# Two halved bias tables moved from the head of VectorE's sequence to just before the first maxima, with a new work order for all engines

## The chip, the cores and the metric

The kernel runs on one core of one Trainium2 chip. Its time is the device time of one execution in microseconds (us). The core has TensorE (PE: matmuls and transposes, its results go to PSUM), VectorE (DVE), ScalarE (ACT), GpSimd (POOL) and SyncE (SP, which here only issues DMAs). Each engine works through its own list of instructions in order, and waits on semaphores for the others.

## What is computed

One transformer layer on x of shape 2 x 1024 x 128, in float32:

```python
x = x + attn(layernorm(x), Wq, Wk, Wv, q_gamma, ..., Wo, bo)   # 16 heads of 8, causal,
                                                               # layernorm per head on q and k, rope, softmax
x = x + ffn(layernorm(x), ...)
# ffn: gate = softmax(x @ gate_w.T); the best 2 of 4 groups, then the best 2 of 16 experts
h1 = einsum('td,edi->tei', xf, We1) + be1
h3 = einsum('td,edi->tei', xf, We3) + be3
yo = einsum('tei,eid->ted', silu(h1) * h3, We2) + be2
y  = einsum('te,ted->td', combine, yo)
z  = silu(xf @ ws1 + bs1) * (xf @ ws3 + bs3) @ ws2 + bs2        # two shared experts
```

All 16 experts are computed for all tokens, as 8 pairs and one unit for the shared experts (9 units of 128 rows), and weighted afterwards. The silu is made of a tanh, with input and one bias halved: tanh((a + b1) / 2), and (c + b3) / 2. The tables of halved biases are `b1h` and `b3h`, 128 x 9 each.

## The kernel before

The 2048 tokens are four tiles x = 0 to 3 of 512 (tiles 0 and 1 are the first halves of the two batches). Attention runs in 16 groups a = 0 to 15 (4 heads of one tile each). A group's maxima come first: `max` (PE, scores of queries against keys), `maxred` (DVE, reduction out of PSUM), `mneg` (POOL), `mturn` (PE), `mcopy` (ACT), `mrow` (SP). Then `scores` (PE), `exp` (ACT), `pv` (PE), `leave` (ACT), `oT` (PE), `oT_read` (DVE). A tile whose attention is done goes through `onT`, `proj` (PE), `proj_read`, `norm2` (DVE), `norm2_apply` (ACT), `x2T` (PE), `gate` (PE), `gate_read`, `route1` to `route3` (DVE), `cT` (PE), `cT_read` (ACT), `cstore` and `cload` (SP: the weights of the experts go to DRAM and come back spread over the partitions), and the units of its experts: `moeV`, `moeU` (PE), `moe_v`, `moe_t` (ACT), `moe_a` (DVE), `moe_g` (POOL), `moe_h` (POOL; for tile 3 `moe_h_dve` on DVE) and `moe_y` (PE, sum over the units), then `y_leave` (ACT), `yturn` (PE), `final` (DVE) and `store` (SP).

There is no scheduler. A text table `ORDER` of 1323 words gives one total order of these stages; each engine walks through it and emits those that are its own (`for kind, arg in SCHEDULE`). A word such as `max.8.2@01` also names the PSUM banks that the stage fills. Moving a word moves the stage within its engine's sequence, and its waits with it.

Ahead of the table's stages SP issues all loads in a fixed list (L501 to L531): the attention weights, the rope tables and biases (`ld_rope`), the masks, tile 1 of x, four padding loads of the stacked keys and queries, tiles 2 and 3 of x, and last the 14 loads of the experts (`ld_moe`), of which the shared bias `bs2` is the last. Tile 0 of x is loaded through ACT's queue (L787). SP's first stage of the table is `stack.0.0.0` (L489), a DMA of the first bf16 parts of the rotated queries.

The head of the sequence goes: `norm.0` (DVE, L1017 on: statistics, a Newton iteration for the square root in ops of 128x4, and the normalised tile) waits only for tile 0 of x; `xT.0`, `qkv.0` to `qkv.3` (PE) and their reads (ACT); `tables.0` (DVE, L1147) waits for `ld_rope`; `norm.1`; `headsum.0`, `headrstd.0`, `rope.0` (DVE); `qT.0`, `kT.0` (PE), their parts and stacks; then the first `max`. For tile 1 POOL makes the rope products (`rope_pool.1`, `rope_join.1`), and `xbo` (POOL, L970) adds the output bias to a tile. The stage `halved` (DVE, L1160 and L1161) makes `b3h` and `b1h`:

```python
dve.wait_ge(ld_moe, 16 * N_MOE)
dve.tensor_scalar(b3h[:, :], b3[:, :], 0.5, None, ALU.mult)
dve.tensor_scalar(b1h[:, :], b1[:, :], 0.5, None, ALU.mult).then_inc(consts, 1)
```

`consts` is waited for by ACT ahead of `moe_v.0.0` and `cT_read.0` alone. In the kernel before `halved.0` is the first word of the table.

Of the kernel before, what the change touches and what calls it, by code (L numbers as in the profile page):

```python
# [134 lines left out]
qkv.10@4 qkv_read.9 qkv.11@3 rope_pool.1 qkv_read.10 stack_act.0.1.2 qkv_read.11 headsum.2 max.0.0@45 max.0.1@23  # L135
maxred.0.0 max.0.2@01 maxred.0.1 max.0.3@45 rope_join.1 maxred.0.2 max.0.4@23 maxred.0.3 max.0.5@01 maxred.0.4
max.1.0@45 maxred.0.5 max.1.1@23 maxred.1.0 xbo.2 norm_apply.3 max.1.2@01 qT.1@6 maxred.1.1 max.1.3@45 mneg.0
maxred.1.2 qT_lead.1 rstd_pool.2 max.1.4@23 stack.1.0.0 maxred.1.3 max.1.5@01 maxred.1.4 mturn.0@5 xT.3@4 mcopy.0
maxred.1.5 xT_read.3 mrow.0 max.2.0@23 kT.1@5 maxred.2.0 qkv.12@4 kT_lead.1 qT_rest.1 max.2.1@01 qkv_read.12
stack.1.1.0 max.2.2@23 maxred.2.1 qkv.13@6 qkv.14@4 stack.1.0.1 maxred.2.2 qkv_read.13 max.2.3@01 kT_rest.1 qkv_read.14  # L140
qT_low.1 max.2.4@23 qkv.15@6 maxred.2.3 stack.1.1.1 kT_low.1 max.2.5@45 qkv_read.15 maxred.2.4 scores.0.0@01 xbo.3
stack.1.0.2 exp.0.0 maxred.2.5 stack.1.1.2 scores.0.1@23 mneg.1 exp.0.1 scores.1.0@01 headsum.3 rope_pool.2 mturn.1@6
max.3.0@45 exp.1.0 max.3.1@23 maxred.3.0 pv.0 mcopy.1 maxred.3.1 mrow.1 scores.1.1@01 max.3.2@45 exp.1.1 scores.2.0@23
maxred.3.2 exp.2.0 max.3.3@01 max.3.4@45 maxred.3.3 pv.1 maxred.3.4 scores.3.0@23 pv.2 exp.3.0 mneg.2 max.3.5@01
rstd_pool.3 leave.0 mturn.2@6 maxred.3.5 max.4.0@45 mcopy.2 scores.3.1@23 mrow.2 maxred.4.0 exp.3.1 oT.0@6 max.4.1@01
oT_read.0 max.4.2@45 maxred.4.1 scores.4.0@23 pv.3 exp.4.0 maxred.4.2 max.4.3@01 scores.4.1@23 maxred.4.3 max.4.4@45
exp.4.1 maxred.4.4 scores.5.0@01 scores.6.0@23 exp.5.0 pv.4 exp.6.0 mneg.3 max.4.5@45 scores.6.1@01 rope_join.2
maxred.4.5 pv.5 exp.6.1 scores.7.0@23 leave.1 mturn.3@6 max.5.0@45 mcopy.3 max.5.1@01 maxred.5.0 exp.7.0 mrow.3 pv.6
# [5 lines left out]
exp.11.0 scores.12.0@01 maxred.6.4 rope_join.3 pv.10 mcopy.5 exp.12.0 pv.11 mrow.5 max.6.5@45 leave.3 max.7.0@23
maxred.6.5 scores.12.1@01 stack.2.0.1 oT.3@6 exp.12.1 maxred.7.0 max.7.1@45 stack.2.0.2 oT_read.3 scores.13.0@01
scores.13.1@23 stack.2.1.2 maxred.7.1 mneg.6 exp.13.0 qT.3@6 exp.13.1 pv.12 qT_lead.3 scores.14.0@01 max.7.2@45
qT_rest.3 exp.14.0 max.7.3@23 pv.13 maxred.7.2 qT_low.3 pv.14 max.7.4@01 maxred.7.3 leave.4 onT.0@6 maxred.7.4
max.7.5@45 onT_read.0 scores.15.0@23 proj.0@6 exp.15.0 maxred.7.5 scores.15.1@01 proj_read.0 scores.16.0@23 exp.15.1
norm2.0 mturn.6@5 oT.4@6 mneg.7 exp.16.0 max.8.0@01 mturn.7@4 mcopy.6 pv.15 mcopy.7 mrow.6 max.8.1@23 kT.3@5 mrow.7
kT_lead.3 maxred.8.0 norm2_apply.0 stack.3.1.0 maxred.8.1 max.8.2@01 x2T.0@4 oT_read.4 kT_rest.3 max.8.3@23 x2T_read.0  # L160
moeV.0.0@4 maxred.8.2 kT_low.3 stack.3.1.1 moeU.0.0@5 moe_v.0.0 maxred.8.3 stack.3.1.2 max.8.4@01 moe_t.0.0 moeV.0.1@4
maxred.8.4 max.8.5@23 moe_v.0.1 moe_a.0.0 gate.0@6 maxred.8.5 moe_g.0.0 max.8.6@45 max.8.7@01 maxred.8.6 moeU.0.1@3
gate_read.0 moeV.0.2@2 moe_t.0.1 maxred.8.7 moe_y.0.0 moe_v.0.2 moe_a.0.1 max.8.8@45 gate_exp.0 max.8.9@01 maxred.8.8
# [10 lines left out]
exp.22.0 moe_y.0.5 moe_h.0.7 exp.22.1 moe_y.0.6 moe_g.0.8 moe_y.0.7 moe_h.0.8 scores.23.0@01 scores.24.0@23 exp.23.0
stack.3.0.1 pv.21 exp.24.0 moe_y.0.8 stack.3.0.2 stack.3.0.0 scores.24.1@01 y_leave.0 scores.25.0@23 pv.22 exp.24.1
exp.25.0 yturn.0@5 scores.25.1@01 final.0 pv.23 exp.25.1 scores.26.0@23 store.0 max.9.3@45 leave.7 maxred.9.3
max.9.4@01 exp.26.0 pv.24 maxred.9.4 max.9.5@45 oT.7@6 maxred.9.5 pv.25 oT_read.7 scores.26.1@01 scores.27.0@23
exp.26.1 max.9.6@45 onT.1@6 maxred.9.6 exp.27.0 pv.26 onT_read.1 max.9.7@45 scores.27.1@01 maxred.9.7 proj.1@6 exp.27.1
# [1075 lines left out]
```

## Time and profile before

| | us |
|---|---|
| median of 3 runs | 449.93 (449.13 to 450.18) |
| the profiled execution, its own time | 447.54 |
| its span, first to last instruction | 445.7 |
| PE busy | 355.9 (80%) |
| DVE busy | 316.7 (71%) |
| ACT busy | 267.3 (60%) |
| POOL busy | 151.8 (34%) |

The profiled execution lies 2.4 us under the median, and 1.8 us of its time lie outside the span. Rows of the trace have the start of an instruction or a merged group in us from the span's start, its length, engine, source line and operation, what it writes and reads, how many, and in brackets how long the engine had been idle and what released it. SPq and ACTq are the issue of a DMA.

### The profile page before, as it was taken

To read this page: it belongs to the slowest core of one execution; us is meant where nothing else is said; L and a number is where in the kernel's file an instruction comes from. 1 tells how busy PE (TensorE), PEld (TensorE's weight loads), DVE (VectorE), ACT (ScalarE), POOL (GpSimd) and SP (SyncE) were. 2 spreads that over 40 slices of the span, in tenths; PEclk is the share of its full clock that TensorE was granted. 3 is DMA by queue.
4 is the path that set the end of the run, shared out by engine and by line. 5 is a ranking of instruction groups with operands and counts; after the bars stand their busy time and mean duration, and the time that the engine had idled before them with its cause. 6 is when DMAs were issued, how large, how long until landed. Compare 5 with 4: busy or idle time off the path is not lost.

```text
span 445.7 us, 8177 instructions
## 1 busy us (share of the span) xinstructions
PE 355.9 (80%) x2999; PEld 154.1 (35%) x2999; DVE 316.7 (71%) x619; ACT 267.3 (60%) x395; POOL 151.8 (34%) x182
## 2 busy tenths in 40 slices
PE   1005445889898999999978998989978699999895
PEld 1002222535454343434422333333432233344332
DVE  0027999997979997527897876888897961136954
ACT  1004433477677477677758268767856479957670
POOL 0003179788871223920135720000000001557252
PEclk9999756799999899999989999999979999999999
DMA  4970040130130202630000800000000001700081
GB/s 122 212 130 1 0 118 24 48 98 2 41 85 26 72 1 53 142 94 3 0 0 13 181 2 1 3 2 25 2 2 0 4 1 28 166 1 0 1 189 50
DMA packets 26424, 21.69 MB, mean 49 GB/s; under 512 B 9201, under 2 KB 22162, under 8 KB 26322
## 3 DMA queue, kind: packets, MB, share of 16 engines
q1 hardware_dynamic: 24994, 20.12, 19.4%
q10 hardware_dynamic: 1392, 1.05, 0.9%
q8 instruction: 25, 0.41, 0.4%
q14 instruction: 13, 0.11, 0.1%
HBM read 13.56 MB, written 1.18 MB: 33 GB/s over the span
## 4 chain that ended last, share of the span: by engine, by line
PE 42%; DVE 39%; SPq 7%; issue 4%; ACT 4%; DMA 2%; POOL 1%; DVEq 0%; ACTq 0%
PE psum L687 11%; DVE mx_diag L1072 11%; DVE mx_full L1072 7%; PE psum L666 6%; PE psum L722 6%; PE psum L733 5%; PE psum L640 4%; PE psum L614 3%; PE psum L596 2%; ACT probs L795 2%; SPq L523 2%; DVE mv L1144 2%; DVE nr L1011 2%; DVE nr L1012 2%; DMA comb_b<-combine_scratch 1%
## 5 line engine op out<-in xcount | busy, mean ns | idle before, releaser
L795 ACT ACTIVATE probs<-psum 128x1024 f32<-128x1024 f32 x144 | 141.6, 1022 | 55.8 <-PE psum L614 29.9
L1072 DVE TENSOR_REDUCE mx_diag<-psum 128x4 f32<-128x512 f32 (+2 forms) x96 | 96.0, 1040 | 18.4 <-PE psum L640 17.9
L1072 DVE TENSOR_REDUCE mx_full<-psum 128x2 f32<-128x1024 f32 x64 | 75.9, 1219 | 12.6 <-PE psum L640 12.3
L994 POOL TENSOR_TENSOR mh<-mh,mv 128x512 f32<-128x512 f32 x36 | 45.4, 1270 | 98.2 <-DVE mv L1144 98.2
L687 PE MATMUL psum<-probs,v_ones 128*9 128x512 f32 (+3 forms) x768 | 78.0, 497 | 1.0 <-ACT probs L795 0.8
L722 PE MATMUL psum<-x2T,w 128*128 128x512 f32 x144 | 72.3, 629 | 2.9 <-ACT mv L832 1.6
L640 PE MATMUL psum<-k_st,q_st 62*128 62x512 bf16 (+3 forms) x384 | 58.4, 337 | 7.2 <-DVE mx_full L1072 4.9
L666 PE MATMUL psum<-q_st,k_st 64*128 64x512 bf16 (+3 forms) x384 | 54.5, 331 | 8.3 <-DVE mx_full L1072 4.0
L614 PE MATMUL psum<-masks 64*128 64x128 bf16 (+2 forms) x896 | 50.7, 213 | 11.7 <-DVE mx_diag L1072 7.7
L1144 DVE SCALAR_TENSOR_TENSOR mv<-psum,b,mv 128x512 f32<-128x512 f32 x36 | 26.5, 747 | 35.1 <-ACT mh L844 34.9
L614 PEld LDWEIGHTS psum<-masks 64*128 64x128 bf16 x896 | 32.7, 95 | 44.7 <-DVE mx_diag L1072 21.2
L952 POOL CAST negmax<-mx_diag 128x16 bf16<-128x16 f32 x16 | 3.1, 196 | 109.2 <-DVE mx_diag L1197 81.1
L733 PE MATMUL psum<-mh,w 128*128 128x512 f32 x72 | 36.2, 614 | 2.7 <-DVE mh L478 1.6
L722 PEld LDWEIGHTS psum<-x2T,w 128*128 128x128 f32 x144 | 25.8, 196 | 31.7 <-issue 16.2
L666 PEld LDWEIGHTS psum<-q_st,k_st 64*128 64x128 bf16 x384 | 16.5, 94 | 55.6 <-ACT probs L795 32.6
L478 POOL TENSOR_TENSOR mh<-mh,comb_b 128x512 f32<-128x512 f32 x24 | 29.9, 1268 | 6.7 <-DMA comb_b<-combine_scratch 6.0
L596 PE MATMUL psum<-ident,sq 128*128 128x128 f32 x16 | 3.5, 361 | 35.4 <-DVE sq L1032 27.8
L841 ACT ACTIVATE mh<-psum,b1h 128x512 f32<-128x512 f32 x36 | 24.7, 686 | 11.7 <-PE psum L722 11.7
L832 ACT ACTIVATE mv<-psum,b3h 128x512 f32<-128x512 f32 x36 | 24.4, 678 | 7.1 <-PE psum L722 7.0
L640 PEld LDWEIGHTS psum<-k_st,q_st 62*128 62x128 bf16 x384 | 19.0, 97 | 27.3 <-DVE mx_full L1072 12.5
L844 ACT ACTIVATE mh<-mh 128x512 f32<-128x512 f32 x36 | 22.7, 630 | 1.1
L687 PEld LDWEIGHTS psum<-probs,v_ones 128*9 128x9 f32 x768 | 13.7, 89 | 26.6 <-issue 20.3
(146 smaller groups left out, 395.4 us busy)
## 6 DMA issues: line engine op xcount, KB each, us to landing
comb_b<-combine_scratch SPq DMA_DIRECT2D x32, 256.0 KB, 5.4
q_st<-parts SPq DMA_DIRECT2D x24, 128.0 KB, 2.3
k_st<-parts SPq DMA_DIRECT2D x18, 128.0 KB, 2.3
w<-in_We SPq DMA_DIRECT2D x3, 512.0 KB
k_st<-in_c_pad SPq DMA_DIRECT2D x2, 512.0 KB, 8.5
out<-xs SPq DMA_DIRECT2D x4, 256.0 KB, 2.3
xs<-in_x SPq DMA_DIRECT2D x3, 256.0 KB, 10.4
k_st<-parts ACTq DMA_DIRECT2D x6, 128.0 KB, 2.7
```

Source lines behind the costliest of these rows:

```text
L478: engine.tensor_tensor(h, h, comb_b[:, u, :], ALU.mult).then_inc(weighted, 1)
L614: return pe.matmul(dst, masks[r, slot, :], blocked, start=start, stop=stop, skip_group_check=True)
L640: last = pe.matmul(w[:, par, i * keys:(i + 1) * keys], q_st[r, x % 2, 2 * g + m, q0:q0 + P], k_st[r, b, 2 * g + m, k0:k0 + keys], start=(w ...
L666: last = pe.matmul(w[:, par, col:col + cols], k_st[rows(par), b, 2 * g + m, kt * P:(kt + 1) * P], q_st[rows(par), x % 2, 2 * g + m, q0:q0 ...
L687: last = pe.matmul(acc[32 * j:32 * j + VC, q0:q0 + cols], v_ones[:, b, kt, G * g + j, :], probs[:, n % P_RING, j % 2, col:col + cols], sta ...
L722: pe.matmul(w, (w1 if kind == "moeU" else w3)[:, unit(n), :], x2T[:, x % 2, :], start=True, stop=True).then_inc(work_full, 1)
L733: last = pe.matmul(y, w2[:, unit(n), :], mh[:, at % T_RING, :], start=(n == 0), stop=(n == UNITS - 1), skip_group_check=True)
L795: act.activation(probs[:, n % P_RING, :, :], wpair("scores", (s, i)), ACT.Exp, scale=SCALE).then_inc(exp_done, 1)
L841: act.activation(t, wbank("moeU", (x, n)), ACT.Tanh, bias=b1h[:, unit(n):unit(n) + 1], scale=0.5).then_inc(act_t, 1)
L994: pool.tensor_tensor(t, t, mv[:, at % V_RING, :], ALU.mult).then_inc(gate_done, 1)
L1072: dve.tensor_reduce(dst[:, a % 2, qt, :, pairs[0]:pairs[0] + nm], w, AX.X, ALU.max, negate=True).then_inc(max_free, 1)
L1144: dve.scalar_tensor_tensor(out=v, in0=wbank("moeU", (x, n)), scalar=b1[:, unit(n):unit(n) + 1], in1=v, op0=ALU.add, op1=ALU.mult).then_inc ...
```

## The change

No instruction is added or removed. `halved.0` leaves the head of the table and stands behind `norm.3`, ahead of `headsum.2` and the first `maxred`. The rest of the table is a new order from there on. Up to `halved.0` every engine has the same sequence as before.

```diff
 ORDER = """
-halved.0 ones.0 ones.1 norm.0 weights.0@6 weights_read.0 weights2.0@5 weights2_read.0 tables.0 xbo.0 xT.0@6 xT_read.0
+ones.0 ones.1 norm.0 weights.0@6 weights_read.0 weights2.0@5 weights2_read.0 tables.0 xbo.0 xT.0@6 xT_read.0 norm.1
...
+qkv.10@4 qkv_read.9 qkv.11@3 rope_pool.1 stack_act.0.1.2 qkv_read.10 qkv_read.11 halved.0 headsum.2 max.0.0@45
...
+moe_v.3.4 final.2 moe_g.3.2 cT.3@2 moe_a.3.3 store.2 moeU.3.4@3 cT_read.3 moe_g.3.3 cstore.3 moeV.3.5@5 moe_t.3.4
```

VectorE at the head of the program (`-` is the kernel before, `+` the changed one; L1019 and L1022 are the first ops of `norm.0`):

```order
 L1153 MEMSET combT 17x512
 L1154 MEMSET psum 128x512
-L1160 TENSOR_SCALAR b3h<-b 128x9
-L1161 TENSOR_SCALAR b1h<-b 128x9
 L1019 BN_STATS stats<-xs 128x6 x4
 L1022 BN_AGGR mean_var<-stats 128x2 x4
```

`norm.0` now follows the two memsets directly, and the wait for the experts' loads has gone from there.

VectorE where the two ops stand now (L1013 and L1036 end `norm.3`, L1041 is `headsum.2`, L1072 the first maxima):

```order
 L1013 SCALAR_TENSOR_TENSOR rstd<-nr,seed 128x4
 L1036 SCALAR_TENSOR_TENSOR shift<-mean_var,rstd 128x4
+L1160 TENSOR_SCALAR b3h<-b 128x9
+L1161 TENSOR_SCALAR b1h<-b 128x9
 L1041 TENSOR_REDUCE ssum<-sq 128x128
 L1072 TENSOR_REDUCE mx_diag<-psum 128x4 x2
```

GpSimd beside that place (L457 and L460 are the end of `rope_pool.1`, L970 is `xbo.2`, L468 and L469 are `rope_join.1`):

```order
 L457 TENSOR_TENSOR sq<-qk,g_cos 128x1024
 L460 TENSOR_TENSOR roped<-qk,g_sin 128x16x32 x2
+L970 TENSOR_TENSOR xs<-xs,bo_b 128x512
 L468 TENSOR_TENSOR sq<-sq,g_add 128x1024
 L469 TENSOR_TENSOR roped<-roped,sq 128x1024
-L970 TENSOR_TENSOR xs<-xs,bo_b 128x512
```

`xbo.2` now comes ahead of `rope_join.1`.

PE near the end of the program, before (L697 is `proj.3`, L596 of w_raw is `x2T.3`, L705 is `gate.3`, L713 is `cT.3`, L722 are `moeV` and `moeU`, L733 and L737 `moe_y`):

```order
L697 MATMUL psum<-w_o,o_normT 128x128 x4
L722 MATMUL psum<-x2T,w 128x512 x6
L733 MATMUL psum<-mh,w 128x512 x3
L596 MATMUL psum<-ident,w_raw 128x128 x4
L733 MATMUL psum<-mh,w 128x512
L705 MATMUL psum<-w_o,x2T 128x16 x4
L722 MATMUL psum<-x2T,w 128x512 x3
L733 MATMUL psum<-mh,w 128x512
L722 MATMUL psum<-x2T,w 128x512 x5
```

The same place after (L596 of yT is `yturn.2`):

```order
L722 MATMUL psum<-x2T,w 128x512 x3
L733 MATMUL psum<-mh,w 128x512 x2
L737 MATMUL psum<-combT,b 128x512
L733 MATMUL psum<-mh,w 128x512 x2
L596 MATMUL psum<-ident,w_raw 128x128 x4
L733 MATMUL psum<-mh,w 128x512 x2
L705 MATMUL psum<-w_o,x2T 128x16 x4
L733 MATMUL psum<-mh,w 128x512 x2
L722 MATMUL psum<-x2T,w 128x512 x4
L733 MATMUL psum<-mh,w 128x512
L722 MATMUL psum<-x2T,w 128x512 x2
L596 MATMUL psum<-ident,yT 128x128 x4
```

Between `x2T.3` and `cT.3` PE has 11 `moeV`, `moeU` and `moe_y` stages of tile 3 and tile 2 besides one ahead of the gate before; now it has 13 and `yturn.2` there, two of the `moe_y` ahead of the gate. `moe_y.2.0`, which stood ahead of the end of attention, comes after it. `yturn.2`, `final.2` and `store.2` come ahead of `cstore.3` on their engines; before they came behind the last `cload`.

In the stretch of tile 0's second norm, PE had `mturn.6 oT.4 max.8.0 mturn.7 pv.15 max.8.1 kT.3 max.8.2` between `scores.16.0` and `x2T.0`. Now it has `pv.15 scores.16.1 scores.17.0 mturn.6 max.8.0 max.8.1 pv.16 max.8.2 mturn.7 pv.17 max.8.3` there. The units of tile 0's experts, which stood among maxima and scores, stand closer together, and `oT.4` and `kT.3` behind them.

## Rows read from the trace of the kernel before

**Rows 1.** The page: busy time, then busy tenths in 40 equal slices.
```profile
PE 355.9 (80%) x2999; PEld 154.1 (35%) x2999; DVE 316.7 (71%) x619; ACT 267.3 (60%) x395; POOL 151.8 (34%) x182
...
DVE  0027999997979997527897876888897961136954
```
**Rows 2.** Waits, first 60 us: engine and work, releaser, us in total, times, longest.
```profile
DVE b3h L1160 <- DMA b<-in_bs: 28.7, 1, 28.7
```
**Rows 3.** Timeline, head: start, length, engine, line, operation.
```profile
0.72 0.47 ACTq L787 DMA_DIRECT2D xs<-in_x  x1
...
6.37 0.43 SPq L508 DMA_DIRECT2D bo_b<-in_bo  x1
...
7.32 0.43 SPq L511 DMA_DIRECT2D xs<-in_x  x1
...
29.25 0.33 SPq L531 DMA_DIRECT2D b<-in_bs  x1
30.73 0.17 DVE L1160 TENSOR_SCALAR b3h<-b 128x9 f32<-128x9 f32 x1 [28.69 <-DMA b<-in_bs]
...
30.88 0.86 DVE L1019 BATCH_NORM_STATS2 stats<-xs 128x6 f32<-128x128 f32 x4
...
35.40 0.17 DVE L1149 COPY gb_rot<-gb 128x16 f32<-128x16 f32 x1
...
38.17 0.87 DVE L1019 BATCH_NORM_STATS2 stats<-xs 128x6 f32<-128x128 f32 x4
...
42.16 0.16 DVE L1036 SCALAR_TENSOR_TENSOR shift<-mean_var,rstd 128x4 f32<-128x4 f32 x1
...
43.96 1.22 DVE L1041 TENSOR_REDUCE ssum<-sq 128x128 f32<-128x1024 f32 x1 [1.64 <-ACT v_ones L815]
```
**Rows 4.** DMA issues: KB each, median us from issue to landing; then line 511 alone.
```profile
xs<-in_x ACTq DMA_DIRECT2D x1, 256.0 KB, 3.6
bo_b<-in_bo SPq DMA_DIRECT2D x1, 64.0 KB, 4.1
out<-xs SPq DMA_DIRECT2D x4, 256.0 KB, 2.3
...
DMA to landing us min/median/max: 5.3/10.4/10.7
```
**Rows 5.** Timeline, first stack DMA to the first maxima.
```profile
57.68 27.70 SPq L489 DMA_DIRECT2D q_st<-parts  x9
...
67.55 2.34 POOL L454 TENSOR_TENSOR qk<-qk,hrstd 128x1024 f32<-128x1024 f32 x1
67.64 2.27 DVE L1012 TENSOR_TENSOR nr<-nr,rstd 128x4 f32<-128x4 f32 x1
...
74.07 1.97 POOL L468 TENSOR_TENSOR sq<-sq,g_add 128x1024 f32<-128x1024 f32 x1
...
75.25 12.12 DVE L1072 TENSOR_REDUCE mx_diag<-psum 128x4 f32<-128x512 f32 x13
...
78.42 1.27 POOL L970 TENSOR_TENSOR xs<-xs,bo_b 128x512 f32<-128x512 f32 x1
```
**Rows 6.** Timeline near the end: a one-input VectorE op beside GpSimd.
```profile
400.62 1.26 POOL L478 TENSOR_TENSOR mh<-mh,comb_b 128x512 f32<-128x512 f32 x1
...
401.08 0.83 DVE L1028 TENSOR_SCALAR rstd<-mean_var 128x4 f32<-128x4 f32 x1
```
**Rows 7.** Stretches: length, busy PE, PEld, DVE, ACT, POOL, clock, DMA share, GB/s.
```profile
140.00:150.00 10.00, 7.92 (x38) 3.23 (x38) 9.05 (x28) 5.68 (x12) 1.57 (x3) 0.83 0.24 70
150.00:160.00 10.00, 9.65 (x68) 4.44 (x66) 9.65 (x15) 5.43 (x10) 2.52 (x2) 1.00 0.04 12
...
340.00:350.00 10.00, 7.48 (x108) 3.02 (x108) 8.68 (x17) 4.96 (x6) 0.42 (x2) 1.00 0.01 3
```
**Rows 8.** Timeline, tail of tile 3.
```profile
411.93 1.02 PE L733 MATMUL psum<-mh,w 128*128 128x512 f32 x2
...
421.64 0.60 PE L713 MATMUL psum<-ident,lg 128*16 128x128 f32 x4 [1.14 <-DVE lg L1138]
```

More of the change, by code:

```diff
@@ L134 @@
 kT_rest.0 stack.0.0.1 xT.2@6 norm.3 stack_act.0.1.1 xT_read.2 qT_low.0 qkv.8@6 qkv.9@5 qkv_read.8 kT_low.0 stack.0.0.2
[L135 to L148, printed above, removed]
@@ L154 @@
[L154 to L163, printed above, removed]
@@ L174 @@
[L174 to L178, printed above, removed]
@@ new lines @@
+norm_apply.3 qT.1@6 maxred.1.3 rstd_pool.2 max.1.5@01 maxred.1.4 mturn.0@5 qT_lead.1 kT.1@4 mcopy.0 stack.1.0.0
+maxred.1.5 kT_lead.1 max.2.0@23 xT.3@5 maxred.2.0 max.2.1@01 xT_read.3 mrow.0 qT_rest.1 max.2.2@23 qkv.12@5 maxred.2.1
+stack.1.1.0 qkv.13@6 qkv_read.12 maxred.2.2 max.2.3@01 qkv_read.13 qkv.14@5 stack.1.0.1 maxred.2.3 max.2.4@23
+qkv_read.14 qT_low.1 kT_rest.1 qkv.15@6 max.2.5@01 maxred.2.4 qkv_read.15 xbo.3 stack.1.1.1 maxred.2.5 kT_low.1
+scores.0.0@23 stack.1.0.2 exp.0.0 headsum.3 scores.0.1@01 mneg.1 stack.1.1.2 rope_pool.2 exp.0.1 scores.1.0@23
@@ new lines @@
+mneg.8 scores.21.1@01 moe_h.0.8 scores.22.0@23 exp.21.1 mturn.8@5 pv.20 mcopy.8 moe_y.0.7 exp.22.0 mrow.8 moe_y.0.8
+leave.6 scores.22.1@01 y_leave.0 pv.21 exp.22.1 max.9.0@45 max.9.1@23 maxred.9.0 pv.22 scores.23.0@01 maxred.9.1
+max.9.2@45 exp.23.0 stack.3.0.1 oT.6@6 maxred.9.2 scores.24.0@23 scores.24.1@01 exp.24.0 stack.3.0.2 pv.23 oT_read.6
+stack.3.0.0 yturn.0@5 leave.7 exp.24.1 scores.25.0@23 final.0 oT.7@6 exp.25.0 max.9.3@45 oT_read.7 store.0 pv.24
+maxred.9.3 scores.25.1@01 scores.26.0@23 exp.25.1 onT.1@6 max.9.4@45 exp.26.0 pv.25 maxred.9.4 onT_read.1
@@ new lines @@
+moe_y.1.1 maxred.10.10 moe_h.1.3 max.10.11@23 moe_h.1.4 max.10.12@45 maxred.10.11 scores.34.1@01 moe_y.1.2 exp.34.1
+maxred.10.12 moe_h.1.5 max.10.13@23 scores.35.0@01 maxred.10.13 pv.34 moe_h.1.6 exp.35.0 mmin.10 max.11.0@45
+max.11.1@23 moe_h.1.7 maxred.11.0 max.11.2@01 moe_y.1.3 mneg.10 maxred.11.1 moe_y.1.4 moe_h.1.8 moe_y.1.5 maxred.11.2
+moe_y.1.6 max.11.3@45 max.11.4@23 maxred.11.3 max.11.5@01 moe_y.1.7 maxred.11.4 moe_y.1.8 mturn.10@5 maxred.11.5
+y_leave.1 scores.35.1@23 mcopy.10 yturn.1@4 exp.35.1 mrow.10 max.11.6@01 final.1 maxred.11.6 scores.36.0@23 store.1
@@ L252 @@
+moeV.3.7@3 moe_t.3.6 cload.3.2 moe_g.3.5 moeU.3.7@2 cload.3.3 moe_v.3.7 moeV.3.8@4 moe_a.3.6 moe_t.3.7 moeU.3.8@3
+moe_g.3.6 moe_h_dve.3.1 moe_v.3.8 moe_h_dve.3.2 moe_y.3.1 moe_t.3.8 moe_h_dve.3.3 moe_h_dve.3.4 moe_h_dve.3.5 moe_y.3.2
+moe_h_dve.3.6 moe_a.3.7 moe_y.3.3 moe_a.3.8 moe_g.3.7 moe_y.3.4 moe_y.3.5 moe_g.3.8 moe_h_dve.3.7 moe_y.3.6
+moe_h_dve.3.8 moe_y.3.7 moe_y.3.8 y_leave.3 yturn.3@5 final.3 store.3
 """
```

186 lines of the change are left out of this document (97 added, 89 removed).

## The prediction, made before the changed kernel ran

> **What bounds the kernel now.** I read the page's busy shares first, then the waits of the first 60 us, then the timeline of the head, and only then the stretches and the tail. The page shows PE busy for 80% of the span and DVE for 71%, so no single engine fills it; but the DVE row of the slices is 0 for the first two slices (22 us) and 2 in the third [rows 1]. The kernel is PE-bound once attention runs, and nothing-bound at its head. The waits name the cause: DVE stood 28.7 us at `b3h`, for the load of the last shared bias [rows 2]. The timeline shows that load issued by SP at 29.25 as the last of the fixed list, `b3h` at 30.73, and `norm.0` behind it at 30.88 [rows 3]. Tile 0 of x, which is all that `norm.0` needs, had been issued at 0.72 and took 3.6 us to land [rows 3, 4]: it lay there from 4.3 on. All further work hangs on `norm.0`, so the wait is on the path in full. What the reader should see is that two ops of 0.17 us hold up the program because their engine works in order, not because anybody needs them: their readers are the experts' units, which need a whole tile's attention first.
>
> **Part 1, the wait leaves the head.** I follow the DVE chain to `headsum.0` (43.96), the first op that needs both DVE's and ACT's work [rows 3]. `norm.0` starts at 0.72 + 3.6 = 4.3 in place of 30.88. It took 35.40 - 30.88 = 4.5 us and the last of its output some 0.1 more: done at 8.9. `tables.0` waits for the rope loads; the last, `bo_b`, is issued at 6.37 and lands 4.1 later, at 10.5 [rows 3, 4]. So a new wait of 1.6 us appears here. The tables took 38.17 - 35.40 = 2.8 us: 13.3. `norm.1` needs tile 1 of x, issued at 7.32; of the three loads of line 511 it is the first and has the minimum of 5.3 us, since the four padding loads come behind it: 12.6, so it does not wait [rows 3, 4]. It took 42.32 - 38.17 = 4.15 us: 17.45. On the other side ACT finished its reads of `qkv.0` to `qkv.3` at 43.96, which is 8.5 us behind `norm.0`: 17.4. `headsum.0` stood 1.64 us idle for ACT before [rows 3]; that slack swallows the new wait for the tables. So `headsum.0` starts at 17.5 in place of 43.96, which is **26.5 us earlier**.
>
> From there to the first maxima at 75.25 [rows 5] the sequences are the same, and the question is which absolute time they run into. SP's list is done at 29.25 + 0.33 = 29.6 [rows 3]. The first stack DMA was issued at 57.68 [rows 5] and moves to 31.2, 1.6 us behind SP's list and 0.5 behind the landing at 30.7. Tiles 2 and 3 of x are issued at about 11 and land 10.7 us later at most [rows 4], near 22, ahead of `norm.2` (after the stacks' start, beyond 30). So nothing of the gain is taken back here. The cover is thin, though: without those 1.6 us of margin every microsecond more is lost. Bounds of this term: 24.5 (SP's list or x late by 2 us) to 26.6 (30.88 - 4.3).
>
> **Part 2, the two ops where they stand now.** They come at 74.2 on the old clock, some 48 on the new: the loads are in since 30.7, there is no wait. Alone they cost 2 x 0.17 = 0.3 us, and DVE is on the path, being busy without a gap into the maxima from 75.25 [rows 5]. But GpSimd works beside them on 128x1024 operands. An op of 128x4 on DVE that starts under such an op lasts until it ends: 2.27 us, against 2.34 of GpSimd's `qk` [rows 5]. That one has two inputs; the nearest row for a one-input TENSOR_SCALAR is 0.83 us, begun 0.46 after a GpSimd op of 1.26 and ending with it [rows 6]. So they block as well. In the new order GpSimd runs `xbo.2` (1.27 us [rows 5]) at 74.07 where `rope_join.1` (1.97) began. `b3h` then waits some 1.2 us, and `b1h` either slips through behind it or waits 1.97 more. Bounds 0.3 to 3.5; I take 2.0, between the two outcomes. It costs on DVE; PE waits for the maxima there anyway.
>
> The Trainium skill, page "SBUF — State Buffer", section "SBUF: two separate sides", says that GpSimd and VectorE share one port pair under an exclusive lock, and that a VectorE op is locked out when it is in a 2-port mode or has two SBUF inputs. If our one-input op ran in no such mode, the price would be the 0.3 us; the row of 0.83 us speaks for the lock.
>
> **Part 3, the new order, middle.** The same stages at the same lengths; only gaps can change. The clearest gap is that of tile 0's second norm: PE was busy 7.92 of 10 us from 140 on and 9.65 in the next stretch [rows 7], so about 1.7 us are lost while `x2T.0` waits. The new order has two `scores` and two `pv` more in that place. I take -1.0 (0 to -1.7). Elsewhere PE's idle share in such a stretch goes up to 2.5 us in the last row there [rows 7], and I can't rank the rest: the closer row of tile 0's experts costs ACT about what PE needs for them. I put 0 with bounds of -4 to +4, some two such stretches closed or opened.
>
> **Part 4, the tail.** A `moe_y` takes 1.02 us, four transposes 0.60 [rows 8]. Between `x2T.3` and `cT.3` PE has two more `moe_y` and `yturn.2`: 2.64 us; `cT.3` waited 1.14 us for DVE's routing [rows 8], so 1.5 us remain. One `moe_y` has left the work ahead of attention's end, -1.0. And `store.2` now is issued just ahead of `cstore.3`: 256 KB that take 2.3 us to land [rows 4] stand before the small store on which the experts' weights depend. Bounds 0 to 2.3; I take 0.5, since `final.2` is ready at about the time of `cT.3`. Sum of the tail +1.0 (-0.5 to +3).
>
> The Trainium skill, page "DMA: Bandwidth & Descriptors", section "Queues, rings and completion order", says that descriptors of one issuing engine are consumed in ring order on each DMA engine. By that the 256 KB are served first and the price would be nearer to the upper bound, +2.3 in place of +0.5; no row here has the two together.
>
> **Sum.** -26.5 + 2.0 - 1.0 + 1.0 = -24.5 us. The profiled execution, 447.54 (span 445.7), would go to 423.0 (span 421.2). The median lies 2.4 above it; from the median 449.93 the forecast is **425.4**.
>
> **Rivals.** *A, the new order fits better than I can see* (it fills gaps of the size of [rows 7] in several stretches): another -5 to -9, 416 to 420. For it: PE idles in nearly every stretch. Against: each such gap ends on DVE, which is busy 71%.
> *B, it fits worse*: another +5.5 to +12, 431 to 437, if tile 0's experts in a closer row starve PE. For it: each unit passes ACT, DVE and GpSimd in turn. Against: PE's work for a unit is as long as ACT's.
> *C, the head gives less*: if the stack DMAs or SP's list are late, or the port holds both ops and more, 3 to 8 us of the gain go: 428 to 433.
> *D, no change*: the freed time is lost at a point that does not move, such as the stacks waiting for the whole load list at a later landing. It would need the list to end near 57; it ended at 29.6 [rows 3]. 450.
> *E, slower*: the experts of tile 0 stand in PE's queue in a row, and the maxima and scores behind them wait. PE idles when a unit's chain (two products, ACT, DVE, GpSimd) is slower than PE's own work for it. If each of the 36 units cost 0.75 us of PE (DVE's op per unit, unhidden), that is 27 us and more than the head gives: 452 or more. It decides from there on, when PE's idle time of today in the attention part nearly doubles. Against: only tile 0's units have clearly moved together, and `mv` and `mh` have several buffers, so that units overlap.
>
> **How the numbers follow.** Forecast (419.5 to 430.5): 0.70. A: 0.13. B: 0.07. C beyond the forecast's range: 0.06. D: 0.015. E: 0.025. The forecast's range adds the bounds roughly in squares: 1.5 for the head, 1.6 for the port, 4 for the middle, 1.8 for the tail, about 4.9 to either side; with the near part of A and of B and C, 419 to 431 holds about 8 in 10. Differences within 0.2% (0.9 us) can't be told from no change: faster 0.96, same 0.015, slower 0.025.
>
> **What would show it.** In the profile after, `norm.0` starts near 4.3 and nothing waits for `b<-in_bs`; DVE waits about 1.6 us at the tables for `bo_b`; `headsum.0` is at 17.5, the first stack DMA at 31.2, the first maxima at about 50.8 rather than 48.8; L1160 and L1161 last together 1 to 3 us. PE's stretch about `x2T.0` is busy 9 of 10. `cT.3` has no wait for DVE, and `combine_scratch` lands later than 1.6 us after issue if `store.2` is ahead. If the span from the first maxima to the end is over 5 us from 445.7 - 75.25 = 370.5, the middle was wrong; if `headsum.0` is later than 20, the head was.

## The result: the head gave what was forecast, the middle gave far more

| kernel | median, us | lowest to highest | profiled execution | its span | its mean clock |
|---|---|---|---|---|---|
| before, beside after | 449.97 | 449.13 to 450.18 (4) | 447.54 | 445.7 | 0.950 |
| after | 416.95 | 416.74 to 419.32 (4) | 416.74 | 414.9 | 0.954 |

The ratio is 0.929 (95% interval 0.926 to 0.932): 33.0 us faster between the medians, 30.8 between the two profiled spans. The forecast was 24.5 us, 425.4, with 419.0 as its lower end. The result lies 2 us below that range, where rival A had put its 416 to 420.

The page of after, busy shares and then DVE and the clock in 40 slices (10.4 us each). Against [rows 1], DVE has work from the first slice on and PE fills 85% of the span; the sum of PE's busy time fell from 355.9 to 352.3 us with the same 2999 matmuls. The clock row has a dent in its first slices and one 8 behind it.

```profile
PE 352.3 (85%) x2999; PEld 153.8 (37%) x2999; DVE 314.9 (76%) x619; ACT 267.0 (64%) x395; POOL 151.3 (36%) x182
...
DVE  4899998878899963789988977698998741265753
...
PEclk9865859999999999999999999999989999999999
```

The same row of before has its dent from the fifth slice on, and behind it 8, 8 and 7, which I had passed over:

```profile
PEclk9999756799999899999989999999979999999999
```

The head, which answers to [rows 3]. The timeline of DVE in after, and SP's queue: start, length, engine, line, operation, and in brackets the wait.

```profile
4.28 0.87 DVE L1019 BATCH_NORM_STATS2 stats<-xs 128x6 f32<-128x128 f32 x4 [2.25 <-DMA xs<-in_x]
...
10.83 0.17 DVE L1149 COPY gb_rot<-gb 128x16 f32<-128x16 f32 x1 [1.94 <-DMA bo_b<-in_bo]
...
13.63 0.86 DVE L1019 BATCH_NORM_STATS2 stats<-xs 128x6 f32<-128x128 f32 x4
...
17.70 1.21 DVE L1041 TENSOR_REDUCE ssum<-sq 128x128 f32<-128x1024 f32 x1
```

```profile
29.87 0.33 SPq L531 DMA_DIRECT2D b<-in_bs  x1
31.37 1.88 SPq L489 DMA_DIRECT2D q_st<-parts  x3
```

`norm.0` starts at 4.28 (said: 4.3), DVE waits 1.94 us at the tables for `bo_b` (said: 1.6), `norm.1` doesn't wait, `headsum.0` starts at 17.70 (17.5), the first stack DMA is issued at 31.37 (31.2). The two halved ops, where they stand now, with GpSimd beside them:

```profile
47.82 1.24 DVE L1160 TENSOR_SCALAR b3h<-b 128x9 f32<-128x9 f32 x1
48.97 0.16 DVE L1161 TENSOR_SCALAR b1h<-b 128x9 f32<-128x9 f32 x1
49.05 1.20 DVE L1041 TENSOR_REDUCE ssum<-sq 128x128 f32<-128x1024 f32 x1
50.17 10.38 DVE L1072 TENSOR_REDUCE mx_diag<-psum 128x4 f32<-128x512 f32 x11
```

```profile
47.76 1.26 POOL L970 TENSOR_TENSOR xs<-xs,bo_b 128x512 f32<-128x512 f32 x1
```

The first maxima are at 50.17 in place of 75.25: 25.1 us. Up to here the sum was right within a microsecond. From there to the end of the span before took 370.4 us and after takes 364.7. The prediction had named its own test for this: over 5 us from 370.5, and the middle was wrong. It is 5.8.

### The profile page after: what moved, and what is told of

The parts are those of the page before. It is cut to its first block, busy times and chain, and to the rows that moved or that the text cites. A ratio compares the mean times of both kernels' runs of the same rounds, so it can differ in the third digit from the quotient of the medians.

```text
span 414.9 us, 8178 instructions
## 1 busy us (share of the span) xinstructions
PE 352.3 (85%) x2999; PEld 153.8 (37%) x2999; DVE 314.9 (76%) x619; ACT 267.0 (64%) x395; POOL 151.3 (36%) x182
## 4 chain that ended last, share of the span: by engine, by line
PE 45%; DVE 35%; ACT 6%; issue 6%; DMA 3%; POOL 2%; SPq 2%; DVEq 0%; ACTq 0%; POOLq 0%
PE psum L687 14%; PE psum L666 8%; DVE mx_diag L1072 7%; DVE mx_full L1072 6%; PE psum L733 5%; PE psum L614 5%; PE psum L640 4%; PE psum L722 4%; ACT probs L795 4%; PE psum L596 4%; DVE mv L1144 2%; DVE nr L1012 2%; POOL mh L994 2%; DVE nr L1011 2%; DMA comb_b<-combine_scratch 2%
## 5 line engine op out<-in xcount | busy, mean ns | idle before, releaser
L1072 DVE TENSOR_REDUCE mx_diag<-psum 128x4 f32<-128x512 f32 (+2 forms) x96 | 95.7, 1038 | 19.0 <-PE psum L640 17.9
L1072 DVE TENSOR_REDUCE mx_full<-psum 128x2 f32<-128x1024 f32 x64 | 75.6, 1217 | 16.9 <-PE psum L640 16.7
L722 PE MATMUL psum<-x2T,w 128*128 128x512 f32 x144 | 69.1, 606 | 1.5 <-ACT mv L832 0.8
L1144 DVE SCALAR_TENSOR_TENSOR mv<-psum,b,mv 128x512 f32<-128x512 f32 x36 | 26.3, 746 | 30.1 <-ACT mh L844 30.0
L733 PE MATMUL psum<-mh,w 128*128 128x512 f32 x72 | 35.4, 612 | 3.7 <-DVE mh L478 2.8
L722 PEld LDWEIGHTS psum<-x2T,w 128*128 128x128 f32 x144 | 25.0, 189 | 30.1 <-issue 18.3
L605 PE MATMUL psum<-w_qkv,xnT 128*128 128x384 f32 x32 | 17.7, 708 | 2.9 <-ACT xnT L801 2.9
```

Source lines behind the costliest of these rows:

```text
L722: pe.matmul(w, (w1 if kind == "moeU" else w3)[:, unit(n), :], x2T[:, x % 2, :], start=True, stop=True).then_inc(work_full, 1)
L733: last = pe.matmul(y, w2[:, unit(n), :], mh[:, at % T_RING, :], start=(n == 0), stop=(n == UNITS - 1), skip_group_check=True)
L1072: dve.tensor_reduce(dst[:, a % 2, qt, :, pairs[0]:pairs[0] + nm], w, AX.X, ALU.max, negate=True).then_inc(max_free, 1)
L1144: dve.scalar_tensor_tensor(out=v, in0=wbank("moeU", (x, n)), scalar=b1[:, unit(n):unit(n) + 1], in1=v, op0=ALU.add, op1=ALU.mult).then_inc ...
```

## Where the rest came from: the two traces side by side

I took the gain (start or end in before less that in after) at steps that both orders have. First maxima 25.1; fifth attention block left (136.6 against 113.5) 23.1; `proj_read.0` 22.9; tile 0's experts done (the eighth block left, 198.7 against 170.3) 28.3; the thirteenth, 324.9 against 297.1, 27.9; the fourteenth, 351.9 against 320.6, 31.4; `x2T.3` read, 407.5 against 375.3, 32.2; the end 30.8. So there are two jumps: 5.4 us in the stretch of tile 0's second norm and experts, 3.5 us in that of tile 2's second norm.

In both places the clock column differs. Stretches of before (length, busy PE, PEld, DVE, ACT, POOL, then the granted clock, DMA share, GB/s):

```profile
144.00:146.00 2.00, 1.17 (x6) 0.74 (x6) 1.97 (x4) 1.17 (x4) 0.00 (x0) 0.84 0.17 44
146.00:148.00 2.00, 1.77 (x6) 0.62 (x5) 1.97 (x4) 0.58 (x1) 0.61 (x1) 0.50 0.54 157
148.00:150.00 2.00, 2.00 (x6) 0.61 (x4) 1.57 (x2) 0.81 (x2) 0.54 (x1) 0.80 0.50 143
...
328.00:330.00 2.00, 0.82 (x6) 0.32 (x4) 2.00 (x3) 0.64 (x1) 0.00 (x0) 0.92 0.00 0
330.00:332.00 2.00, 1.80 (x14) 0.82 (x14) 1.86 (x6) 1.63 (x3) 0.00 (x0) 0.50 0.03 8
332.00:334.00 2.00, 2.00 (x10) 0.15 (x9) 1.87 (x8) 1.61 (x2) 0.00 (x0) 0.50 0.00 0
```

and PE's timeline in the first of them:

```profile
144.77 0.39 PE L640 MATMUL psum<-k_st,q_st 62*128 62x512 bf16 x2 [1.80 <-DVE mx_full L1072]
145.22 1.01 PE L596 MATMUL psum<-ident,w_raw 128*128 128x128 f32 x4
...
147.00 2.84 PE L722 MATMUL psum<-x2T,w 128*128 128x512 f32 x4 [0.23 <-ACT x2T L801]
```

Read it like this: PE stands 1.80 us for DVE; from 145.4 on the clock is at 0.50 (1.2 of 2.4 GHz), four transposes take 1.01 us in place of 0.63 to 0.66, and four expert products take 2.84 us, 0.71 each (the clock is back at 148.8, within them). After has in the same place a pause too, but of 0.61 us, and a clock of 1.00; its experts' products take 0.49 each:

```profile
122.94 0.63 PE L596 MATMUL psum<-ident,w_raw 128*128 128x128 f32 x4 [0.61 <-ACT maxT L906]
...
124.52 1.07 PE L705 MATMUL psum<-w_o,x2T 128*128 128x16 f32 x8
125.43 1.96 PE L722 MATMUL psum<-x2T,w 128*128 128x512 f32 x4
```

The pause costs once; what follows it costs again, without PE being idle there. A caution on the two jumps: only 3.4 us at half clock lie in the first of them, and 6.8 against 3.4 in the second, so that the clock column alone can't fill both; a later section comes back to this. Hence two theories. **K**: the gain over the forecast is time at half clock that no longer occurs, and whoever keeps PE busy in the pause gets it in any order. **G**: it is the gaps themselves that the order closes. And before these, whether it is the order at all (**O**), or the shift by 25 us that moved the work to other places of whatever sets the clock (**S**).

## Experiments

**Head and order apart.** In the order of before, one word moved:

```diff
-halved.0 ones.0 ones.1 norm.0 ...
+ones.0 ones.1 norm.0 ... kT_rest.0 stack.0.0.1 xT.2@6 norm.3 halved.0 stack_act.0.1.1 ...
```

> The order of before with one word moved: the two halved ops stand behind norm.3 in place of at the head. Theory O (what I missed is the new order: it closes holes in PE's row, and with them half-clock stretches): this kernel has the head's gain alone, 25.1 us at the first maxima, and nothing more, so 423 to 426 us; its trace keeps stretches of granted clock 0.50 after the second norms of tiles 0 and 2. Theory S (the shift itself did it: the same order, begun 25 us earlier, runs with fewer half-clock stretches): 417 to 419 us, and the stretches at 0.50 are gone with the old order too.

Measured 426.92 us (423.79 to 428.76), 22.9 less than the 449.77 of before beside it.

```diff
-ones.0 ones.1 norm.0 weights.0@6 ... qkv_read.11 halved.0 headsum.2
+halved.0 ones.0 ones.1 norm.0 weights.0@6 ... qkv_read.11 headsum.2
```

> The new order with the two halved ops put back at the head. Theory O: the order alone is worth the 5.7 us that the profiled spans show behind the first maxima, up to 8 if the medians' part is the order's too: 442 to 444 us. Theory S: the order is worth nothing by itself, 448 to 450 us.

Measured 441.93 us (441.20 to 442.97), 7.8 less (ratio 0.983, 0.978 to 0.987). So O holds and S falls: the order by itself is worth 7.8 us, at the old place of the halved ops. The two parts add up to 30.7 of the 33.0. The first came out 1 us above what O had said, and its executions lie 5 us apart; the next sections give a likely reason for both.

**Which half of the order.** After's order up to `leave.7`, then before's, and the reverse, both with the halved ops moved.

> Halved moved; the new order up to leave.7 (the experts of tile 0 done), and from there the old one. Theory O: the gain at leave.7 was 28.3 us and at the first maxima 25.1, so this part of the order is worth 3.2: about 421.5 us, 3 below the old order with halved moved, and no half-clock stretch near the x2T.0 hole, but one near the second norm of tile 2. Theory S: like the old order with halved moved.

Measured 423.77 us (423.24 to 424.89), 2.3 above the 421.5 expected. And its trace has the clock at 0.50 from 126.2 to 129.7, behind `x2T.0`, where none was expected: up to `leave.7` its sequence is that of after, whose clock stood at 1.00 there.

> Halved moved; the old order up to leave.7, and from there the new one. Theory O: the rest of the order is worth 5.7 - 3.2 = 2.5 us: about 422.5 us, with a half-clock stretch behind x2T.0 and a shorter one near the second norm of tile 2. Theory S: like the old order with halved moved.

Measured 420.04 us (418.91 to 421.19). Against the 426.92 of the old order the first half is worth 3.2, which is the difference expected, and the second 6.9, where I expected 2.5. Together that is 10.0, and from 426.92 to after it is 10.0. The halves add up, but their sizes are not those of the two profiled executions.

**The half clock itself.** In the old order with the halved ops moved: nine matmuls of 128x512 in bf16 that compute nothing, in the pause ahead of `max.8.2`. They write the bank that `x2T.0` fills next and overwrites.

```diff
+KEEP = {("max", (8, 2)): ("x2T", 0, 9)}
 for kind, arg in SCHEDULE:
+    if (kind, arg) in KEEP:
+        name, at, count = KEEP[kind, arg]
+        spare = fill(name, at)
+        for _ in range(count):
+            pe.matmul(spare, ident_bf[:, :], masks[:, 0:4, :].rearrange("p n q -> p (n q)"),
+                      start=True, stop=True, skip_group_check=True)
```

> The old order with halved moved, and 9 spare bf16 matmuls (128x512, about 0.21 us each, into the bank that x2T.0 fills next, which overwrites them) just ahead of max.8.2, where PE waited 1.80 us for DVE at 121.2 and behind which the clock stood at 0.50 from about 120.9 to 128.6. Theory K (PE's pause costs little, the half clock behind it costs half of its length): the clock stays at 1.00 there, 7.7 us of it, and the time falls by 3 to 4 us against the old order with halved moved, 426.9 to about 423.5, although work was added. Theory G (the pause itself is what the order closes): nothing changes, or PE's queue comes some 0.1 us later: 427.

Measured 422.77 us (422.40 to 423.18): 4.15 less than the 426.92 without them (3.7, if each is taken against the kernel before beside it), and all of its executions are below all of the other's. Work was added, nothing moved. PE in the old order with halved moved, first without and then with the spare matmuls (line 746, lines behind it are 7 further down):

```profile
121.18 0.39 PE L640 MATMUL psum<-k_st,q_st 62*128 62x512 bf16 x2 [1.80 <-DVE mx_full L1072]
121.62 1.11 PE L596 MATMUL psum<-ident,w_raw 128*128 128x128 f32 x4
...
123.50 2.90 PE L722 MATMUL psum<-x2T,w 128*128 128x512 f32 x3 [0.23 <-ACT x2T L801]
```

```profile
118.82 2.11 PE L746 MATMUL psum<-masks 128*128 128x512 bf16 x9
120.86 0.39 PE L640 MATMUL psum<-k_st,q_st 62*128 62x512 bf16 x2
121.23 0.66 PE L596 MATMUL psum<-ident,w_raw 128*128 128x128 f32 x4
...
122.65 1.96 PE L722 MATMUL psum<-x2T,w 128*128 128x512 f32 x4 [0.34 <-ACT x2T L808]
```

and the clock of the stretches that follow, again without and with:

```profile
120.00:122.00 2.00, 0.77 (x4) 0.50 (x5) 2.00 (x2) 1.57 (x5) 0.00 (x0) 0.88 0.02 6
122.00:124.00 2.00, 1.77 (x7) 0.94 (x6) 1.93 (x6) 0.59 (x1) 0.21 (x1) 0.50 0.70 197
124.00:126.00 2.00, 2.00 (x3) 0.67 (x2) 1.97 (x2) 0.41 (x1) 0.94 (x1) 0.50 0.39 110
126.00:128.00 2.00, 2.00 (x5) 0.38 (x4) 0.16 (x1) 0.96 (x2) 0.00 (x0) 0.50 0.31 95
```

```profile
120.00:122.00 2.00, 1.97 (x13) 0.82 (x10) 1.97 (x4) 1.25 (x5) 0.00 (x0) 1.00 0.17 45
122.00:124.00 2.00, 1.66 (x5) 0.69 (x5) 1.97 (x4) 0.72 (x2) 0.60 (x1) 1.00 0.57 164
124.00:126.00 2.00, 2.00 (x8) 0.45 (x6) 2.00 (x3) 1.79 (x3) 0.55 (x1) 1.00 0.25 66
126.00:128.00 2.00, 1.85 (x15) 1.29 (x14) 2.00 (x3) 0.69 (x1) 0.55 (x1) 1.00 0.45 131
```

The expert products go from 0.97 us each to 0.49. K holds in this place: from the first maxima to the eighth block left, the two traces take 126.1 us (10.2 of it at half clock, 3.4 of them at 97) and 122.7 us (none). The Trainium skill, page "TensorE: Matmul & The Clock Gate", section "Why this matters for your kernels", warns of idle gaps between bursts that let the clock fall. The rows agree that it falls behind idle time. The longest single pause here, 1.80 us, is shorter than the gaps that the page names.

The same nine matmuls in the kernel before itself:

> The kernel before, with nothing moved, and 9 spare matmuls ahead of max.8.2, as in the kernel with the old order and halved moved. Its clock stood at 0.50 from about 145.3 to 149.6 behind this pause, and the same edit took 4.15 us off the old order with halved moved. Theory K: 2 to 4 us faster than before, 446 to 447.5. Theory G: 449 to 450.

Measured 447.51 us (445.58 to 448.53, 10 executions) beside 448.99 (17 executions); ratio 0.9967 (0.9945 to 0.9990). That is 1.5 us, with an interval of 0.5 to 2.5, and less than the 2 to 4 I gave it. The stretch there was 3.4 us long, so half of it, 1.7, is what K should have said; 4.15 had been measured where it was twice as long. The two profiled spans are equal (445.9 and 445.7), although this execution has 3.4 us less at half clock (10.2 against 13.6, one stretch at 354 being new). So the factor of a half doesn't hold for this pair of traces.

**More spare work, in the maxima.** There PE has no free bank ahead of its pauses, so the spare matmuls write the bank of the step itself, once it is free:

```diff
+KEEP = {("max", (8, 2)): ("x2T", 0, 9), ("max", (14, 6)): ("max", (14, 6), 2), ("max", (14, 7)): ("max", (14, 7), 2),
+        ("scores", (59, 0)): ("scores", (59, 0), 2), ("scores", (59, 1)): ("scores", (59, 1), 2)}
```

> As the kernel with 9 spare matmuls, and 2 more (0.43 us) behind the bank wait of each of max.14.6, max.14.7, scores.59.0 and scores.59.1, where PE stood 0.4 to 0.6 us for DVE four times and the clock then stood at 0.50 for 7.5 us (305.9 to 313.3). Theory K: another 3 us less, about 420.5. Theory G: 427, or up to 1 us more for the spare work.

Measured 422.36 us (421.75 to 422.87), only 0.4 less than without these eight; K had said 3. The half clock near 305 is gone in the trace, but one at 217 is there in its stead. That the spare work, which now stands between the maxima, delays DVE is my reading of the rest; no run here shows it by itself.

```diff
+KEEP = {("scores", (59, 0)): ("scores", (59, 0), 3), ("max", (14, 8)): ("max", (14, 8), 3)}
```

> The new order as in after, with 3 spare matmuls (0.64 us) behind the bank wait of scores.59.0 and of max.14.8, the two pauses of 0.69 and 0.78 us ahead of its only half-clock stretch in the middle (301.9 to 305.3). Theory K: this stretch goes, -1.7 us, 415.2. Theory G: 417.0 or 0.5 more.

Measured 416.72 us (415.05 to 420.88), against 416.95 of after: no difference, and so inconclusive. Its four executions took 420.88, 415.05, 417.66 and 415.78 us at mean clocks of 0.935, 0.955, 0.943 and 0.959. In the profiled one, the slowest, the stretch near 302 is gone. But behind `x2T.0`, on rows that are those of after up to 124.9 us (0.36 us later), the clock fell where it had not in after:

```profile
123.30 0.63 PE L596 MATMUL psum<-ident,w_raw 128*128 128x128 f32 x4 [0.61 <-ACT maxT L913]
...
124.56 0.39 PE L640 MATMUL psum<-k_st,q_st 62*128 62x512 bf16 x2 [0.31 <-DVE mx_full L1079]
124.88 1.54 PE L705 MATMUL psum<-w_o,x2T 128*128 128x16 f32 x8
```

The eight products that took 1.07 us in after take 1.54 here, with the same pauses ahead; the clock stood at 0.50 from 125.3 to 132.1. Two more traces have after's instructions up to here: that with the order of before from `leave.7` on and that with `store.2` moved (below); in both the clock fell too, at 126.2 and at 125.9. So the pauses make a fall possible, not certain; it differs from execution to execution of the same instructions.

**One number for all kernels.** For every profiled execution I took the time from the first maxima to the end of the span, and the sum of (1 - clock) / 0.5 over stretches of 1 us (from 16 us behind the first maxima, where the head's slow start is over, to 6 us ahead of the end), which is the time at half clock. At half clock a product takes twice its time (0.97 against 0.49 us above), so a PE that bounds loses half of it; where another engine bounds, less is lost.

| kernel | first maxima to end | at half clock | first less half of second |
|---|---|---|---|
| before | 370.4 | 13.6 | 363.6 |
| old order, halved moved | 376.8 | 26.4 | 363.6 |
| new then old | 372.6 | 17.1 | 364.1 |
| old then new | 368.9 | 13.7 | 362.1 |
| new order, halved at the head | 364.7 | 3.4 | 363.0 |
| after | 364.7 | 3.4 | 363.0 |
| old order, halved moved, 9 spare | 370.0 | 10.2 | 364.8 |
| the same and 8 more | 370.6 | 6.8 | 367.2 |
| after, 6 spare | 369.3 | 11.3 | 363.6 |
| before, 9 spare | 370.4 | 10.2 | 365.3 |
| new order, halved behind `maxred.0.4` | 364.7 | 3.4 | 363.0 |
| after, `store.2` moved | 367.8 | 13.7 | 361.0 |
| new order, halved behind `maxred.0.4`, 12 spare | 364.2 | 3.4 | 362.5 |
| the same, 11 spare, one pause earlier | 364.1 | 3.4 | 362.4 |

The times from the first maxima differ by 13 us, the last column, for the eight kernels without spare work, by 3. By this sum the old and the new order are 0.6 us apart (363.6 and 363.0), and 5.1 of the order's 5.7 us are clock. But the factor of a half is no more than a rule. Pairs of traces of one order give it directly: before and the old order with halved moved 6.4 us for 12.8, so 0.5; after and its variant with 6 spare 4.6 for 7.9, 0.6 (1.3 us of spare work in it); after and that with `store.2` moved 3.1 for 10.3, 0.3; before and the same with 9 spare nothing for 3.4. With 0.3 in place of 0.5 the clock's share of the 5.7 us is 3.1. So at least about half of the order's gain is clock, perhaps nearly all; these single executions don't say more.

Cut at the eighth block left, the traces show where the order itself counts. From the first maxima to there before took 123.4 us with 3.4 at half clock, before with 9 spare 122.9 with none, and after 120.2 with none. Of these 3.2 us 0.5 went with the half clock, and 2.7 stayed with the clock at 1.00 on both sides: this part is the order's own, by G. From there to the read of `x2T.3` it was 208.8 us with 10.3 at half clock in before and 204.9 with 3.4 in after; there the 6.9 us fewer at half clock are worth 2.1 to 3.4 of the 3.9.

**The price of the two ops beside GpSimd.** The new order with them behind the fifth read of maxima, `maxred.0.4`:

```diff
-qkv_read.10 qkv_read.11 halved.0 headsum.2 max.0.0@45 ...
+qkv_read.10 qkv_read.11 headsum.2 max.0.0@45 ... max.0.5@01 maxred.0.4 halved.0
```

> The new order with the two halved ops four maxima reads later, behind maxred.0.4, where GpSimd's joined rope (2.34 us) is still running or just over. If the 1.24 us that L1160 took beside GpSimd's xbo.2 was on the path, and GpSimd is idle where they stand now, the gain is about 1.1 us: 415.8. If they fall under the 2.34 us op, they hold DVE up to 2.3 us, and the time is 0 to 1 us over after.

Measured 415.98 us (415.03 to 417.07). The time alone doesn't part it from after; the trace does:

```profile
47.40 0.16 DVE L1036 SCALAR_TENSOR_TENSOR shift<-mean_var,rstd 128x4 f32<-128x4 f32 x1
47.48 1.21 DVE L1041 TENSOR_REDUCE ssum<-sq 128x128 f32<-128x1024 f32 x1
48.61 4.67 DVE L1072 TENSOR_REDUCE mx_diag<-psum 128x4 f32<-128x512 f32 x5
53.20 0.16 DVE L1160 TENSOR_SCALAR b3h<-b 128x9 f32<-128x9 f32 x1
53.27 0.16 DVE L1161 TENSOR_SCALAR b1h<-b 128x9 f32<-128x9 f32 x1
```

Both ops now take 0.16 us, and `headsum.2` follows `norm.3` at once. In after they held it up from 47.82 to 49.05, so they cost 1.2 us there and cost 0.15 here (53.20 to 53.35): 1.1 us to be had.

**The store in the tail.** In the new order `store.2` moved behind `cload.3.3`.

> The new order with store.2 moved behind cload.3.3. If its 256 KB ahead of the small store hold this one up, the time from the issue of combine_scratch to the issue of its first read back falls from the 1.88 us of after towards the 1.66 of before, and by no more than 0.3 us; if the queue had cost what I allowed at most, 2.3 us, after would have shown 3.9, so that is out already. The time itself: 415 to 417.5.

One execution, 419.29 us at a clock of 0.941, which says nothing of an edit of this size. In its trace the first read back of the experts' weights is issued 1.71 us behind the small store, in after 1.88:

```profile
390.80 0.39 SPq L557 DMA_DIRECT2D out<-xs  x1
391.47 0.60 SPq L545 DMA_DIRECT2D combine_scratch<-combT  x1
393.35 5.20 SPq L553 DMA_DIRECT2D comb_b<-combine_scratch  x8
```

```profile
394.21 0.32 SPq L545 DMA_DIRECT2D combine_scratch<-combT  x1
395.92 4.54 SPq L553 DMA_DIRECT2D comb_b<-combine_scratch  x7
```

So 256 KB issued 0.67 us ahead of the small store delay it by 0.2 us in this pair, not by the 2.3 of its own landing. All traces together say a little more: this step took 1.88 to 2.15 us in the seven that have `store.2` ahead, and 1.57 to 1.71 in six of the seven that don't (2.16 in the other), so 0.3 us is the usual price.

**All of it together.** The new order, the halved ops later, and spare matmuls:

```diff
+KEEP = {("max", (8, 2)): ("max", (8, 2), 2), ("max", (8, 3)): ("max", (8, 3), 2), ("max", (8, 4)): ("max", (8, 4), 2),
+        ("scores", (59, 0)): ("scores", (59, 0), 3), ("max", (14, 8)): ("max", (14, 8), 3)}
```

> The new order, the two halved ops behind maxred.0.4, and 2 or 3 spare matmuls behind the bank waits of max.8.2, 8.3, 8.4, scores.59.0 and max.14.8. Theory K: both half-clock stretches that the executions of the new order show now and then (behind 124 and behind 300) are gone in all of them: 414 to 415 us, and the times lie closer together than the 415.0 to 420.9 seen without it. Theory G: as with the halved ops later alone, 416.0, or 1 us more for the work added.

Measured 414.61 us; five of six executions between 413.94 and 414.96, one at 417.00; ratio to before 0.924 (0.921 to 0.927). That is 2.3 us under after, of which 1.1 is the halved ops' by the trace; the new order with these ops later and no spare work has a ratio of 0.925 (0.920 to 0.929), so that the spare matmuls by themselves are not clear of noise. The stretch near 297 was still there, since the clock fell behind a pause just ahead of the spare work. One pause earlier:

```diff
-        ("scores", (59, 0)): ("scores", (59, 0), 3), ("max", (14, 8)): ("max", (14, 8), 3)}
+        ("max", (14, 6)): ("max", (14, 6), 2), ("max", (14, 7)): ("max", (14, 7), 2), ("scores", (59, 0)): ("scores", (59, 0), 1)}
```

> As the kernel with the halved ops later and five spare fills, but the spare matmuls near the second norm of tile 2 stand one pause earlier: 2 each behind the bank waits of max.14.6 and max.14.7 and 1 behind that of scores.59.0, since with the later ones the clock fell at 296.7, behind a pause of 0.96 us, before they ran. Theory K: the last half-clock stretch of 3.4 us in the middle goes, 1.7 us less than 414.6: about 413. If it stays, or DVE then waits for the spare work, 414.5 to 415.5.

Measured 415.15 us (413.12 to 417.34). The stretch near 297 is gone:

```profile
290.00:300.00 10.00, 9.16 (x91) 4.09 (x83) 9.86 (x10) 6.33 (x11) 0.42 (x2) 1.00 0.02 4
300.00:310.00 10.00, 8.10 (x80) 2.86 (x80) 9.28 (x32) 7.03 (x10) 0.00 (x0) 1.00 0.00 0
...
214.00:218.00 4.00, 4.00 (x26) 0.53 (x18) 1.37 (x2) 2.61 (x4) 0.00 (x0) 0.67 1.04 243
```

and this execution has one of the same length near 213 instead. The gain that K promised for it, 1.7 us, didn't come in the median; the ratio to before is 0.924 (0.919 to 0.929), the same as without the shift. Filling the pauses one by one reaches its end here; which of the remaining pauses brings the clock down in a given execution I can't foretell from these traces.

## The prediction, step by step

**What bounds the kernel, Part 1 (the wait leaves the head).** Right. 26.5 us were summed for `headsum.0`, 26.3 measured (43.96 to 17.70); the new wait at the tables was 1.9 rather than 1.6, since `bo_b` landed in 4.4 us. The early stack DMA waited for nothing new, and the thin cover of SP's list held.

**Part 2 (the two ops beside GpSimd).** The mechanism was right, the size was not: 1.2 us for the 2.0 taken. Of the two outcomes, 1.2 and some 3.2, the lower one occurred: `b3h` waited for the end of `xbo.2` (both end at about 49.0), and `b1h` slipped through at 0.16 us. A mean between two outcomes was no outcome. The Trainium skill, page "SBUF — State Buffer", section "SBUF: two separate sides", would let a one-input op pass unless it runs in a 2-port mode; the 1.24 us against 0.16 us of the same op elsewhere show that this one was held.

**Part 3 (the middle).** This is the step that failed. From the first maxima (25.1 us gained) to the read of `x2T.3` (32.2) 7.1 us were gained where the sum had 2.0: 1.0 for the middle, and the 1.0 that the tail term had for a `moe_y` gone from ahead of the end of attention, which falls on this side of the cut. I priced the gap at `x2T.0` by PE's idle time alone, "about 1.7 us", out of [rows 7]; the same row has the clock, 0.83 over 10 us. That is 3.4 us at half clock, up to another 1.7 us, in a stretch in which PE was busy and which I took for full. Nor did I look for other stretches with a clock under 1.00; two more, 3.4 us at 230 and 6.8 at 329, lay in before's trace. All three together are 13.6 us, and after has 3.4 left. So a term was put at nothing without a reason, the time at half clock. By the factor of a half the difference is worth 5.1 us, and the 2.0 that remain are what the sum had for the order; by the 0.3 that one pair of traces gives it is worth 3.1, and 4.0 remain for filled gaps. The experiment with nine spare matmuls shows that such a stretch costs time by itself; how the 7.1 us divide is worked out from single traces and stays open within these bounds.

In rival A I named gaps and DVE's share as the reason. Its range held the time, in part by luck: filled gaps account for 2 to 4 us of the 7.1, the 2.7 us up to the eighth block left being the clearest, and the clock for the rest.

**Part 4 (the tail).** Sized well, for partly wrong reasons. From the read of `x2T.3` to the end 1.4 us were lost, where the terms on this side of the cut were +1.5 and +0.5. Up to `cT.3` it was 0.8 for the 1.5, behind it 0.6 for the 0.5. `cT.3` did wait for DVE, 0.78 us, where I said it wouldn't: not for the routing, which ended at 389.52 just as PE came free, but for an op on `mv` behind it. The store ahead of the small one cost 0.2 to 0.3 us, not 0.5. (Before has 12 stages of experts between `gate.3` and `cT.3`, not the 11 of the description; with the one ahead of the gate that makes 13 against 15, and the difference of two on which the sum rests holds.) The Trainium skill, page "DMA: Bandwidth & Descriptors", section "Queues, rings and completion order", as I applied it, would have cost 2.3.

**From the profiled execution to the median.** The spans differ by 30.8 us, the medians by 33.0. Before's profiled execution was one of its fastest, 447.54 us at a mean clock of 0.950; others took up to 451.98 us at 0.939. I added its distance from the median, 2.4 us, to the changed kernel as if it were a constant. Most likely it is time at half clock in the other executions: of 38 further executions of before, those with a mean clock of 0.943 or less took 449.77 us or more, those with 0.950 or more at most 449.15. The new order has less of it: after's profiled execution lies 0.2 us under its median. No trace of a slower execution of before was taken. These 2.2 us, with Part 3's 5.1, Part 2's 0.8 and 0.6 in the tail, less 0.2 in the head, are the 8.5 us by which the forecast was too high.

**The rivals B to E** did not occur. For C, the head gave its 26.3 us and nothing waited for SP's list; for B and E, tile 0's experts in a closer row did not starve PE (7.81 us busy of 8 from 124 on):

```profile
124.00:132.00 8.00, 7.81 (x30) 3.68 (x30) 7.65 (x19) 5.53 (x11) 1.28 (x1) 1.00 0.01 2
```

**Open.** What in the old order with halved moved raises its time at half clock to 26.4 us, from 13.6 with the same order 25 us later, is not settled. The trace is of one execution, the slowest of its four, and executions of this kernel lie 5 us apart. It would explain why moving the halved ops alone gave 22.9 us where the head gives 25.
